# The second stack's planes behind ACT's copies, and planes written out in DRAM: a fused convolution and involution kernel

## The reference, cut to what matters

```python
x = x + _L0_conv_ref(_gn(x), L0_conv_weight, L0_conv_scale)
x = x + _L1_conv_ref(_gn(x), ...)
# _L1_conv_ref, K = 7, G = 16 groups of D = 4 channels:
r = relu(bn(einsum('oc,bchw->bohw', w_r, x)))
ker = einsum('oc,bchw->bohw', w_s, r) + b_span            # 49 taps for each group and pixel
for ki in range(K):
    for kj in range(K):
        out = out + xp[:, :, :, ki:ki + H, kj:kj + W] * ker[:, :, ki * K + kj][:, :, None]
```

## Time and profile before

| | |
|---|---|
| Median of 3 runs | 1944.62 us (1939.90 to 1957.48) |
| Profiled execution | 1947.81 us |
| Its span | 1945.9 us |
| PE busy | 1615.7 us (83%) |
| DVE busy | 1377.2 us (71%) |
| ACT busy | 1054.9 us (54%) |
| POOL busy | 1016.5 us (52%) |
| Moved by DMA | 410.67 MB, 211 GB/s |
| Patch loads | 1120 of 224 KB, 7.1 us from issue to landing (median) |

### The profile page before, as it was taken

How to read it: one execution, slowest core, us unless ns; L and a number is a source line. 1 busy time by engine, 2 the same in 40 slices (tenths; PEclk the granted TensorE clock), 3 DMA queues, 4 the chain that set the end, 5 groups by cost and what they waited for, 6 DMA issues and landing times.

```text
span 1945.9 us, 38822 instructions
## 1 busy us (share of the span) xinstructions
PE 1615.7 (83%) x15072; PEld 730.2 (38%) x15072; DVE 1377.2 (71%) x1699; ACT 1054.9 (54%) x758; POOL 1016.5 (52%) x904
## 2 busy tenths in 40 slices
PE   3488897979889798897978889798897978889785
PEld 2233443434344343343434344343343433344342
DVE  6476786858678686786858678676786858678574
ACT  2355566555656455565545656454565545656443
POOL 1145565454655555465554655555565454655573
PEclk8699998999999899998989999898998999999897
DMA  3669899797998979799797998979799797988992
GB/s 108 166 168 242 187 261 217 189 245 175 253 211 229 231 192 245 183 260 208 204 229 187 257 199 238 226 188 241 188 254 215 197 236 181 254 206 227 208 248 85
DMA packets 211592, 410.67 MB, mean 211 GB/s; under 512 B 83822, under 2 KB 131231, under 8 KB 207263
## 3 DMA queue, kind: packets, MB, share of 16 engines
q1 hardware_dynamic: 136144, 356.79, 73.1%
q10 hardware_dynamic: 75264, 51.39, 10.2%
HBM read 310.30 MB, written 84.93 MB: 203 GB/s over the span
## 4 chain that ended last, share of the span: by engine, by line
POOL 49%; issue 42%; PE 2%; SPq 2%; DVE 2%; DMA 2%; ACT 1%; POOLq 1%; ACTq 0%; DVEq 0%
POOL folded L361 49%; SPq L301 1%; PE ybank L508 1%; POOLq L360 1%; SPq L283 0%; DMA patches<-parts_dram 0%; PE ybank L567 0%; DMA xs<-x_dram 0%; DVE rowsums L730 0%; DVE prod L788 0%; DMA parts_dram<-parts 0%; PE ybank L537 0%; PE ybank L548 0%; ACT patches L428 0%; ACT sgn L381 0%
## 5 line engine op out<-in xcount | busy, mean ns | idle before, releaser
L361 POOL TENSOR_TENSOR folded<-prod 128x448 f32<-128x448 f32 x896 | 1010.8, 1141 | 911.7 <-DVE prod L788 910.9
L788 DVE TENSOR_TENSOR prod<-ybank,relu 128x896 f32<-128x896 f32 x896 | 960.9, 1088 | 405.7 <-PE ybank L567 336.3
L567 PE MATMUL ybank<-patches,wspan 128*64 128x448 f16 x7168 | 863.2, 383 | 240.8 <-ACT patches L428 106.0
L428 ACT ACTIVATE patches<-patches 96x1792 f16<-96x1792 f16 x448 | 736.6, 1689 | 554.7 <-DMA patches<-parts_dram 273.7
L567 PEld LDWEIGHTS ybank<-patches,wspan 128*64 128x64 f16 x7168 | 400.2, 117 | 757.2 <-issue 421.7
L508 PE MATMUL ybank<-sgn,convw 128*128 128x448 bf16 x1008 | 206.4, 358 | 21.4 <-ACT sgn L381 17.0
L585 PE MATMUL obank<-folded,esum 128*32 128x448 f32 x1792 | 214.8, 551 | 1.5 <-POOL folded L361 1.5
L578 PE MATMUL obank<-patches,wbias 128*32 128x448 f16 x3584 | 197.1, 363 | 0.0
L508 PEld LDWEIGHTS ybank<-sgn,convw 128*128 128x128 bf16 x1008 | 93.7, 98 | 135.3 <-issue 31.5
L578 PEld LDWEIGHTS obank<-patches,wbias 128*32 128x32 f16 x3584 | 87.1, 98 | 103.8 <-issue 50.9
L746 DVE SCALAR_TENSOR_TENSOR xs<-ybank,scale,xs 128x896 f32<-128x896 f32 x64 | 66.0, 1032 | 74.9 <-PE ybank L508 74.8
(11 more groups left out here) (90 smaller groups left out, 378.0 us busy)
## 6 DMA issues: line engine op xcount, KB each, us to landing
patches<-parts_dram SPq DMA_DIRECT2D x1120, 224.0 KB, 7.1
parts_dram<-parts SPq DMA_DIRECT2D x128, 256.0 KB, 5.4
xs<-x_dram SPq DMA_DIRECT2D x16, 1568.0 KB, 9.7
sums_dram<-osb ACTq DMA_DIRECT2D x112, 224.0 KB, 6.2
rows<-sums_dram ACTq DMA_DIRECT2D x112, 224.0 KB, 6.7
out_dram<-xs SPq DMA_DIRECT2D x16, 1568.0 KB, 5.9
relu<-blocks SPq DMA_DIRECT2D x256, 49.0 KB
patches<-gb_dram SPq DMA_DIRECT2D x1, 784.0 KB
```

Of the source, the lines that this page charges most:

```text
L361: pool.tensor_tensor(folded[:, u % 8, :], prod[:, u % 2, 0, :], prod[:, u % 2, 1, :], ALU.add).then_inc(fold_done, 1)
L428: act.activation(X2[0:COPIED_ROWS, e % 2, at], X1[0:COPIED_ROWS, e % 3, at], ACT.Copy).then_inc(copied, 1)
L567: mm = pe.matmul(bank("unit", p, n)[64 * t:64 * t + 64, h, 0:N], wspan[:, stack, g, h, :], of_group(e, stack, g), start=(stack == 0), stop ...
L788: dve.tensor_tensor(prod[:, u % 2].rearrange("m h (n c) -> m h n c", c=GC), bank("unit", p, n)[:, :, 0:N].rearrange("m h (n c) -> m h n c" ...
```

## The change: what it does

- The planes are written out in DRAM: D0 holds for each column eight planes of 2048 values side by side, D1 the two low planes of the second stack. A quarter goes out in six DMAs (ten for k = 0, whose runs are cut at the front); a part that is in several planes is written several times, by a source that repeats it.
- The first stack is one DMA of 128 partitions with plane q of tap column r on partition 8 r + q. The selection constants follow this order.
- ACT copies all 128 partitions of X1 to X2, in pieces at units 0 to 3 of a group. The two low planes (`LOADED`, partitions 3 and 7 of every eight) are then loaded over the copied rows: `second_stack` waits on SP for the four copies. One plane of X2 is a copy that has no weights.
- SP sends first_stack(e + 2) ahead of second_stack(e + 1). `spread` and the load of the pair after next move to s = 5. At the start `second_stack(0)` comes behind `spread(0)` and `first_stack(1)`.
- `rsum` has memory of its own, and the waits between it and V are gone. `gather(e - 1)` moves to unit 4, the rows follow two groups behind at unit 3, and the second `arrange` moves from n = 13 to 15.

```diff
--- before.py
+++ after.py
-PLANES = (((0, 0, 32, 4), (0, 4, 0, 2), (0, 1, 33, 4), (1, 0, 96, 2),
-           (0, 2, 34, 4), (1, 1, 1, 2), (0, 3, 35, 4), (1, 2, 97, 2)),
-          ((0, 0, 32, 4), (0, 4, 0, 2), (0, 1, 33, 4), (0, 2, 34, 4), (0, 3, 35, 4),
-           (1, 3, 96, 2), (1, 4, 97, 2)))
-COPIED_ROWS, COPIED_PLANES = 96, 5
+PLANES = (((0, 0), (0, 2), (0, 4), (1, 1), (0, 1), (0, 3), (1, 0), (1, 2)),
+          ((0, 0), (0, 2), (0, 4), (1, 3), (0, 1), (0, 3), None, (1, 4)))
+Q = 8
+
+LOADED = (3, 7)
...
-FIRSTLOAD, SECONDLOAD = 16 * 8, 16 * 2
+FIRSTLOAD, SECONDLOAD = 16, 16 * 2
 COPY = JY * 128
-DWRITE = 16 * 2
+DWRITE = (16 * 10, 16 * 6)
...
-ARRANGE1_AT, ARRANGE0_AT = 13, 46
-SUMS_B, BIAS, SUMS_A, ROWS_AT = 3, 6, 7, 7
-
-COPY_AT = {0: 0, 1: 1, 4: 2, 5: 3}
+ARRANGE1_AT, ARRANGE0_AT = 15, 46
+SUMS_B, ROWS_AT, GATHER, BIAS, SUMS_A = 3, 3, 4, 6, 7
+
+COPY_AT = {0: 0, 1: 1, 2: 2, 3: 3}
...
-        rsum = V[:].rearrange("p y b g c -> p (y b g c)")[:, 0:PX * 2 * HW // POS].rearrange("p (x n) -> p x n", x=PX)
+        rsum = sb("rsum", [128, PX, 2 * HW // POS])
...
-        D = nc.dram_tensor("parts_dram", (2, 2, 128, PART), F16, kind="Internal").ap()
+
+        D0 = nc.dram_tensor("planes_dram", (2, 128, Q, RUN), F16, kind="Internal").ap()
+        D1 = nc.dram_tensor("planes2_dram", (2, 128, 2, RUN), F16, kind="Internal").ap()
...
             def parts_out(p, k):
 
+
                 sp.wait_ge(low_done, 4 * p + k + 1)
                 if p > 0:
-                    sp.wait_ge(d_written[k], DWRITE * p)
-                for l in range(2):
-                    sp.dma_start(D[p % 2, l].rearrange("m (y h n) -> m y h n", y=2, h=4)[:, :, k, :],
-                                 Ev[:, l, k % 2]).then_inc(d_written[k], 16)
-
-            def plane(e, l, a):
+                    sp.wait_ge(d_written[k], DWRITE[k > 0] * p)
+                b = p % 2
+
+                def run(dram, planes, q, l, y, shift, many):
+
+                    src = Ev[:, l, k % 2, y]
+                    if k == 0:
+                        for i in range(many):
+                            cut = BLOCK * (shift + i)
+                            sp.dma_start(dram[b, :, q + i, 0:4 * BLOCK - cut], src[:, cut:]).then_inc(d_written[k], 16)
+                        return
+                    dst = bass.AP(tensor=dram.tensor, offset=(128 * b * planes + q) * RUN + BLOCK * (4 * k - shift),
+                                  ap=[[planes * RUN, 128], [RUN - BLOCK, many], [1, 4 * BLOCK]])
+                    sp.dma_start(dst, src.unsqueeze(1).broadcast_to((128, many, 4 * BLOCK))).then_inc(d_written[k], 16)
+
+                run(D0, Q, 0, 0, 0, 0, 3)
+                run(D0, Q, 4, 0, 1, 0, 2)
+                run(D0, Q, 6, 1, 0, 0, 2)
+                run(D0, Q, 3, 1, 1, 0, 1)
+                run(D1, 2, 0, 1, 1, 1, 1)
+                run(D1, 2, 1, 1, 0, 2, 1)
+
+            def stack(dram, e):
 
                 p = e // E
-                first = ((p % 2) * 2 + l) * 128 * PART + 4 * JX * (e % E) * PART
-                return bass.AP(tensor=D.tensor, offset=first + (a % 2) * (CY // 2) * 128 + (a // 2) * 128,
-                               ap=[[PART, 16], [4 * PART, JX], [1, JY * 128]])
+                return bass.AP(tensor=dram.tensor, offset=(128 * (p % 2) + 4 * JX * (e % E)) * Q * RUN,
+                               ap=[[RUN, 128], [4 * Q * RUN, JX], [1, JY * 128]])
 
             def first_stack(e):
                 if e >= 3:
                     sp.wait_ge(y_ready, GP * (e - 2))
                     sp.wait_ge(first_in[e % 3], FIRSTLOAD * (e // 3))
                 for k in range(4):
-                    sp.wait_ge(d_written[k], DWRITE * (e // E + 1))
-                for l, a, row, step in PLANES[0]:
-                    sp.dma_start(X1[row:row + 15 * step + 1:step, e % 3, :],
-                                 plane(e, l, a)).then_inc(first_in[e % 3], 16)
+                    sp.wait_ge(d_written[k], DWRITE[k > 0] * (e // E + 1))
+                sp.dma_start(X1[:, e % 3, :].rearrange("p (j n) -> p j n", j=JX), stack(D0, e)).then_inc(first_in[e % 3], 16)
 
             def second_stack(e):
+
+                sp.wait_ge(copied, JX * (e + 1))
                 if e >= 2:
-                    sp.wait_ge(y_ready, GP * (e - 1))
                     sp.wait_ge(second_in[e % 2], SECONDLOAD * (e // 2))
-                for l, a, row, step in PLANES[1][COPIED_PLANES:]:
-                    sp.dma_start(X2[row:row + 15 * step + 1:step, e % 2, :],
-                                 plane(e, l, a)).then_inc(second_in[e % 2], 16)
+                p = e // E
+                for i, q in enumerate(LOADED):
+                    src = bass.AP(tensor=D1.tensor, offset=(2 * (128 * (p % 2) + 4 * JX * (e % E)) + i) * RUN,
+                                  ap=[[2 * RUN, 16], [8 * RUN, JX], [1, JY * 128]])
+                    sp.dma_start(X2[q:128:Q, e % 2, :].rearrange("p (j n) -> p j n", j=JX), src).then_inc(second_in[e % 2], 16)
...
             first_stack(0)
-            second_stack(0)
             spread(0)
             first_stack(1)
+            second_stack(0)
             for p in range(pairs):
                 for s in range(E):
                     e = E * p + s
+                    if e + 2 < EALL:
+                        first_stack(e + 2)
                     if e + 1 < EALL:
                         second_stack(e + 1)
-                    if e + 2 < EALL:
-                        first_stack(e + 2)
                     if p + 1 < pairs:
                         if s == 3:
                             parts_out(p + 1, 0)
@@ -337,10 +358,11 @@
                         if s == 4:
                             parts_out(p + 1, 2)
                             parts_out(p + 1, 3)
+                        if s == 5:
                             spread(p + 1)
                     if s == 2 and p > 0:
                         store(p - 1)
-                    if s == 3 and p + 2 < pairs:
+                    if s == 5 and p + 2 < pairs:
                         if p > 0:
                             sp.wait_ge(stored, STORE * p)
                         sp.wait_ge(x_loaded, XLOAD * (p + 2))
@@ -396,15 +418,13 @@
...
                     act.wait_ge(r_spread, SPREAD * p)
-                if p >= 2:
-                    act.wait_ge(out_ready, 4 * (p - 1))
                 act.activation(rsum[:, k, :].rearrange("m (n b) -> m b n", b=2),
                                bank("red", p, k)[:, :, 0:HW // POS],
...
-            def copy_high(e, j):
+            def copy(e, j):
 
                 act.wait_ge(first_in[e % 3], FIRSTLOAD * (e // 3 + 1))
                 if e >= 2:
                     act.wait_ge(y_ready, GP * (e - 1))
                 at = slice(COPY * j, COPY * (j + 1))
-                act.activation(X2[0:COPIED_ROWS, e % 2, at], X1[0:COPIED_ROWS, e % 3, at],
-                               ACT.Copy).then_inc(copied, 1)
+                act.activation(X2[:, e % 2, at], X1[:, e % 3, at], ACT.Copy).then_inc(copied, 1)
...
-                act.wait_ge(r_spread, SPREAD * min(p + 1 + (group % 2 == 0), pairs))
...
-                    if n % GP == SUMS_B and e > 0:
+                    if n % GP in COPY_AT and e + 1 < EALL:
+                        copy(e + 1, COPY_AT[n % GP])
+                    if n % GP == ROWS_AT and e > 1:
+                        rows(e - 2)
+                    if n % GP == GATHER and e > 0:
                         gather(e - 1)
-                    if n % GP in COPY_AT and e + 1 < EALL:
-                        copy_high(e + 1, COPY_AT[n % GP])
-                    if n % GP == ROWS_AT and e > 0:
-                        rows(e - 1)
...
+            rows(EALL - 2)
             gather(EALL - 1)
             rows(EALL - 1)
             arrange(2 * pairs - 1)
...
-                for part, a, row, step in PLANES[stack]:
+                for q, plane in enumerate(PLANES[stack]):
+                    if plane is None:
+                        continue
+                    part, a = plane
 
                     sel = stack if part or stack == 0 else 2
                     for r in range(16):
                         ky, kx = 2 * a + r % 2 - dy, r // 2 - dx
                         if 0 <= ky < K and 0 <= kx < K:
-                            c[ky * K + kx, C_SEL + 384 * pos + 128 * sel + row + step * r] = 1
+                            c[ky * K + kx, C_SEL + 384 * pos + 128 * sel + Q * r + q] = 1
```

5 lines of the change are left out of this document (3 added, 2 removed).

## The result

The changed kernel takes 2008.03 us (median of 4 runs, 2004.27 to 2010.38) against 1944.18 beside it: 1.0315 times, 95% interval 1.0261 to 1.0368. Its profiled span is 2008.5 us, 62.6 more than before. Where it went is read from the first products on DVE. The table has the mean length of each group over the pairs 1 to 14 (of 0 to 15), in us; the last three columns are the length of a pair, the last pair, and the time of the very first product. The forecast of a pair is before's less 0.1, and the groups beside it add up to 116.2 by rounding; that of the first product is 98 for PE's first unit and the 2.7 us that before has from there.

The account below looks back on a forecast made before the run. It took PE to be held in s5 and s6 by patch loads and ACT's copies, behind SP's relu sends and the queue. 1945.9 - 2 (pairs) + 10 (start) - 10 (last pair) = 1943.9 of span, 1943 us on the median; range 1870 to 2030.

Parts of the forecast that it names:

- The wide load: First stack's eight plane loads become one DMA of 128 partitions: 5.0 us of queue for 8.2, 3.2 less.
- C: Rival: the single load is no faster than eight, each stack costing 3.2 us more; about 2050 us, chance 0.12.
- s0 to s3: First four of a pair's seven groups of eight units: no change, planes landing before they are needed.
- At the start: PE's first unit goes from 82.64 to about 98 us; 5 of the 15 made good in group 0: +10.
- The last pair: Where no next pair is prepared: 79.5 us in place of 91.5, of which 10 counted: -10.
- s4: Fifth group of a pair: planes for s5 land at 14.3, needed at 14.7; 16.0 us for 15.7 to 15.9.
- A: The new order works as followed group by group, planes queueing behind a first stack: 1943 us, chance 0.38.
- rival D: ACT's high parts wait for longer writes, holding PE: +2 in s4, +1.5 in s5; 1995 us, chance 0.23.
- s5 and s6: Last two groups of a pair: 35.0 us together, where 36.0 in the pair read and 35.2 over all.
- Own relu buffer, orders of ACT: nothing: The relu buffer of its own, and ACT's rows and gather moved behind the copies: costed at nothing.
- B: Rival: the writes are not held up, s5 under 14 us, -4.5 us a pair; 1875 us, chance 0.27.

Follow-up runs that it names:

- a3: The changed kernel, from the third pair on without the repeated planes for quarters 1 to 3 (output not the reference's): 1963.6 us, ratio 1.011.
- c1: The changed kernel with the next pair's transposes, high and low parts at units 25, 27, 32, 34 in place of 28, 30, 34, 36: 2060.4 us, ratio 1.061.
- e2: The kernel before with only rsum in memory of its own and its waits with V gone: 1948.7 us, ratio 1.002.

## Why the prediction was wrong

**Right.** The wide load is faster (2.5 us of engine time a stack; 3.2 had been counted). When the queue is nearly free a first stack lands 7.1 to 8.8 us after its issue, a little over the 7 that was set as the mark and clear of the 10 that would have said C. s0 to s3 came as forecast. At the start PE's first unit is at 95.42 us where about 98 was forecast; the first product is 11.9 us later than before, where about 15 were forecast, and group 0 gives 3.8 of it back, for 5: +8.1 for +10. The last pair is 10.1 us shorter, for 10 (its working gave 12, and a part was held back by judgement). In s5 the events came in the forecast order.

**s4, the first failed term: 16.0 forecast, 18.2 measured (+2.2 of the 4.4 us a pair).** The working of A followed SP and the queue and said that ACT's third copy waits for the high part, but it put at nothing the time until that high part may begin. The tile of parts has two slots, so the fourth quarter's high part waits for the landing of the second quarter. This was issued up to 894.6, 4.4 us into s4 as forecast, and landed at 898.4, 8.2 into s4; the high part follows at 898.48, DVE's low part behind it, and PE idles until 900.81. PE's waits for low parts are 25.8 us in 15 times, 1.7 us a pair, all in s4, one in each, where before has none; with fewer bytes in the writes (a3) they are 8.6 and s4 is 1.0 us shorter. It is the mechanism of rival D in its place, PE waiting for DVE's low parts, with its price of +2; D's time, 1995, was the nearest of the four. The row for it stood in the kernel before (the third high part idle 3.08 us for the writes, at the start), and A used it for the start only. c1 shows this wait from the other side: earlier quarters only lengthen it.

**s5 and s6, the second: 35.0 forecast, 37.2 measured.** The times below are us after s5 began; the means are of the pairs 1 to 13, in which an image is loaded, and the last column is the pair shown above, which is later than most. The end of the relu rows and of the load is that of their last DMA packets in the trace (3136 and 12544 bytes each).

| | forecast | mean | pair shown |
|---|---|---|---|
| last quarter landed | 6.2 | 5.3 | 6.9 |
| planes for s6 landed | 15.8 | 16.0 | 16.8 |
| first product of s6 | 16.5 | 18.0 | 18.7 |
| last relu send issued | 20.0 | 19.5 | 20.9 |
| relu rows through the queue | no term | 22.4 | 24.5 |
| image load through | 24.3 | 26.7 | 28.4 |
| planes for the next s0 landed | 33.7 | 35.6 | 38.0 |
| first product of the next s0 | 35.0 | 37.5 | 40.0 |

The failed step is that the 16 relu sends were counted as SP's time alone, though their data have to pass too. They need another 2.9 us after the last one is issued, and the load comes behind them. The windows 922 to 945 of the pair shown (same columns) have the low rate while the sends run out, and what follows:

```profile
922.00:930.00 8.00, 5.30 (x34) 3.18 (x36) 3.16 (x3) 6.45 (x4) 2.03 (x2) 0.60 0.70 143
930.00:937.00 7.00, 7.00 (x82) 3.29 (x84) 6.20 (x7) 0.63 (x1) 5.02 (x6) 1.00 0.97 333
937.00:945.00 8.00, 1.47 (x16) 0.27 (x10) 1.09 (x1) 1.26 (x1) 1.96 (x2) 0.82 1.04 328
```

The other terms held: the load takes 4.3 us for 4.3, stack and planes to their landing 8.9 for 8.4. The second error is the step from the landing to the first product. The kernel before has 1.75 us between PE's start and this product; the forecast left 0.7 in s5 and 1.3 at the end of s6, and both are 1.9 to 2.0. In s5 that only moves time between s5 and s6, since the sends follow the writes and not s6's start; at the end it is 0.6 us a pair.

**Slips in its sums, and luck.** Two sums are 1.0 us larger than their terms: 6.2 + 5.0 + 1.0 is 12.2 and not 13.2, and 20.0 + 4.3 + 5.0 + 2.0 + 0.8 is 32.1 and not 33.1. Without the second the forecast would have been 15 us lower, about 1928, and further off; it hid a third of the missing term. That the planes for s6 landed almost when forecast is luck in the same way. By the ceiling of 16 ports, 435 GB/s in the Trainium skill (SBUF — State Buffer, "Door 1: The DMA port swizzle"), the estimate for a stack is 4.2 us and not 4.4; nothing hangs on it.

**Right for a reason that the runs moved.** "Own relu buffer, orders of ACT: nothing" holds for the buffer (e2). The net of the whole, nearly nothing, was a sum of large parts: -64 for the load, +152 for the writes and +179 for the waits, each alone. They don't add (+267 against +64), so the balance that the prediction saw in s5 and s6 was real in kind, but each microsecond a pair is 15 us of the total, and small errors decided the sign. B failed: s5 is 18.0 and not under 14.
